# A memset behind every indirect DMA of GpSimd, and source rows taken from PSUM in one step of a graph network

## What is computed

```python
h = relu(layernorm(x)); x = x + L0(h)   # sum of h[src] * edge_weight * weight per destination
h = relu(layernorm(x)); x = x + L1(h)   # bilinear messages of dst rows and 8 edge features, silu, summed by source
h = relu(layernorm(x)); x = x + L2(h)   # 16x16 matrix of the edge's relation (90) times h[src], times a scalar
h = relu(layernorm(x)); x = x + L3(h)
# L3:
w = (gelu(gelu(edge_attr @ W1 + b1) @ W2 + b2) @ W3 + b3).reshape(-1, 16, 16)
for i in range(4):
    msg = einsum('ei,eio->eo', nodes[src], w)
    nodes = gelu(segment_sum(msg, dst) * inv_deg + nodes @ root_W[i] + root_b[i])
```

## Time and profile before

| what | value |
|---|---|
| median of 3 runs | 23921.9 us |
| the profiled execution | 23937.52 us |
| its span, first to last instruction | 23935.6 us |
| mean granted clock of TensorE | 0.931 |
| instructions | 398,392 |
| PE busy | 20518.6 us (86%) |
| POOL busy | 18138.0 us (76%) |
| DVE busy | 17386.4 us (73%) |
| ACT busy | 14285.8 us (60%) |

### The profile page before, as it was taken

The page is one execution under the profiler, slowest core; times in us unless marked ns, Lnnn a source line. Parts: engine busy times, 40 slices in busy tenths (PEclk is TensorE's granted clock), DMA queues, the critical chain, the costliest instruction groups (busy, mean ns, idle before and its releaser), DMA issues. The chain is left out here.

```text
span 23935.6 us, 398392 instructions
## 1 busy us (share of the span) xinstructions
PE 20518.6 (86%) x109882; PEld 11859.6 (50%) x109882; DVE 17386.4 (73%) x29340; ACT 14285.8 (60%) x24676; POOL 18138.0 (76%) x17163
## 2 busy tenths in 40 slices
PE   7999668888887999996888888699996999879997
PEld 4555345555555666663444444344443444434443
DVE  6555468888887999994555555588886888868886
ACT  7888611111112666663444444488886888878886
POOL 6777778888886777777777777777777777777777
PEclk9999879999998999998998899899998999989998
DMA  3222235555553223332333333366665666656665
GB/s 104 42 43 42 42 76 94 94 94 94 94 93 76 79 78 79 79 76 91 113 114 112 115 114 115 118 200 200 199 200 155 200 201 200 194 161 200 200 200 151
DMA packets 2201224, 2951.16 MB, mean 123 GB/s; under 512 B 782486, under 2 KB 1686884, under 8 KB 2199588
## 3 DMA queue, kind: packets, MB, share of 16 engines
q1 hardware_dynamic: 1340898, 2758.80, 35.2%
q0 software_dynamic: 790944, 162.36, 9.5%
q10 hardware_dynamic: 69282, 28.92, 0.5%
HBM read 2275.75 MB, written 672.64 MB: 123 GB/s over the span
## 5 line engine op out<-in xcount | busy, mean ns | idle before, releaser
L772 POOL DMA_INDIRECT got<-table,idx x14310 | 13886.3, 970 | 4697.2 <-issue 4166.5
L788 PE MATMUL in_place<-place_hot,tparts 128*128 128x512 fp8e4 (+1 forms) x49950 | 10826.1, 375 | 1229.7 <-ACT place_hot L993 1225.6
L993 ACT ACTIVATE place_hot<-place_b,far_lanes 128x512 fp8e4<-128x512 f16 (+1 forms) x17550 | 10584.3, 683 | 9.1 <-PE in_place L788 9.0
L788 PEld LDWEIGHTS in_place<-place_hot,tparts 128*128 128x128 bf16 x49950 | 4905.3, 100 | 6515.0 <-issue 1645.5
L1597 POOL DMA_INDIRECT added<-rows,add_idx x2160 | 3600.4, 1667 | 714.3 <-issue 655.8
L1169 DVE TENSOR_TENSOR prod<-w_in,rows_p 128x2048 f32<-128x2048 f32 x810 | 1853.0, 2288 | 1010.2 <-ACT rows_p L981 972.0
L1640 PE MATMUL acc<-hot,spread 128*128 128x392 bf16 x12960 | 2531.2, 349 | 0.0
L1214 DVE TENSOR_TENSOR prod<-wcopy,got 128x1024 f32<-128x1024 f32 x810 | 983.7, 1230 | 1840.7 <-DMA got<-table,idx 1303.3
L1223 DVE TENSOR_REDUCE msg<-prod 128x64 f32<-128x1024 f32 x1620 | 1967.8, 1215 | 41.3
L1182 DVE TENSOR_REDUCE msg<-prod 128x128 f32<-128x2048 f32 x810 | 1853.1, 2288 | 105.5
L857 PE MATMUL wmat<-k,h 128*128 128x256 f32 x6480 | 1797.6, 402 | 0.0
(11 more groups left out here) (249 smaller groups left out, 21238.2 us busy)
## 6 DMA issues: line engine op xcount, KB each, us to landing
w_in<-kept SPq DMA_DIRECT2D x2430, 512.0 KB
kept<-wcopy SPq DMA_DIRECT2D x810, 512.0 KB, 2.6
got<-table,idx POOLq DMA_INDIRECT x14310
attr<-in_edge_attr SPq DMA_DIRECT2D x270, 768.0 KB
place_b<-place_row SPq DMA_DIRECT2D x1080, 128.0 KB
range_b<-range_row SPq DMA_DIRECT2D x1080, 128.0 KB
rows<-in_src_row SPq DMA_DIRECT2D x270, 512.0 KB
sums<-outb SPq DMA_DIRECT2D x1350, 96.0 KB
```

The source lines that it names most:

```text
L772: pool.indirect_dma_start(out=got[:, r, j * W:(j + 1) * W], out_offset=None, in_=table, in_offset=bass.IndirectOffsetOnAxis(ap=idx[:, r, j ...
L788: mm = pe.matmul(in_place[b][:, h, :], tparts[:, s, t, :], place_hot[:, b, t, h * XC:(h + 1) * XC], start=(t == 0 and s == 0), stop=(t == ...
L993: ins = act.activation(place_hot[:, b, t, :], place_b[:, b, :], ACT.Abs_reciprocal_sqrt, bias=SB["far_lanes"][:, t:t + 1], scale=HOT_SLOPE ...
```

## The change

POOL clears one column of a scratch tile `spacer` behind each indirect DMA at lines 772, 1597 and 1917, a column of its own for each within the ring; before it begins a chunk whose columns were used before, it waits on `spaced` for those memsets. In "kernel_net" ACT copies the 12 gathered rows of a chunk to one PSUM tile, `rows_p`, after the chunk's second `copy_out`; DVE's products read that tile; POOL waits for `rows_made` in place of `got_used`. The bank comes from `h2p`, which has one buffer instead of two, so `layer2` waits for the gelu of the group just before.

```diff
+        spacer = sb("spacer", [P, RING * J0])
...
-            h2p = [ps(f"h2p{k}", [P, GE]) for k in range(2)]
+            h2p = ps("h2p", [P, GE])
+            rows_p = ps("rows_p", [P, 512])[:, 0:J0 * W]
...
                     if at is None or at >= RING:
-                        if kind == "kernel_kept":
+                        if kind in ("kernel_net", "kernel_kept"):
                             pool.wait_ge(S["rows_made"], k - RING + 1)
                         else:
                             pool.wait_ge(got_used[r], q)
                     pool.wait_ge(S["idx_made"], k + 1)
 
+                    if at is None or at >= RING:
+                        pool.wait_ge(S["spaced"], k - RING + 1)
                     pool.sem_inc(S["turn_open"], 1)
                     for j in range(J0):
                         pool.indirect_dma_start(
...
+                        ins = pool.memset(spacer[:, r * J0 + j:r * J0 + j + 1], 0.0)
+                    ins.then_inc(S["spaced"], 1)
...
-                    pe.wait_ge(S["h2_ready"], i * TURN_GROUPS + n + 1)
-                    pe.matmul(h2p[n % 2][:, :], SB["k2"][:, :], h1[:, n % 2, :], start=True, stop=True).then_inc(S["h2_made"], 1)
+                    pe.wait_ge(S["h2_ready"], i * TURN_GROUPS + n + 2)
+                    pe.matmul(h2p[:, :], SB["k2"][:, :], h1[:, n % 2, :], start=True, stop=True).then_inc(S["h2_made"], 1)
...
+                    def rows_over(k, r, q, first):
+
+                        act.wait_ge(got_in[r], (q + 1) * (16 * J0))
+
+                        if not first:
+                            act.wait_ge(w_used, k * GROUPS + 2)
+                        act.activation(rows_p, got[:, r, 0:J0 * W], ACT.Copy).then_inc(S["rows_made"], 1)
+
+                    def turn(i, odd, q, first):
...
                             copy_out(i, n, first)
+                            b, g = divmod(n, GROUPS)
+                            if g == 1:
+                                rows_over(i * HALVES + b, odd * HALVES + b, q, first and b == 0)
...
-                    dve.wait_ge(got_in[r], (q + 1) * (16 * J0))
+                    if kind == "kernel_net":
+                        dve.wait_ge(S["rows_made"], k + 1)
+                        rows_x = rows_p.rearrange("p (j f) -> p j f", f=W)
...
-                            bcast(rows_v[:, g * G:(g + 1) * G, 0:D], 2, D), ALU.mult).then_inc(w_used, 1)
+                            bcast(rows_x[:, g * G:(g + 1) * G, 0:D], 2, D), ALU.mult).then_inc(w_used, 1)
...
-                    dve.sem_inc(got_used[r], 1)
+                    if kind == "relational":
+                        dve.sem_inc(got_used[r], 1)
...
+        spacer = sb("spacer", [P, HALVES * ADDED])
...
+                        if at is None or at >= HALVES:
+                            pool.wait_ge(S["spaced"], k - 1)
                         for tables in (range(0, half), range(half, ADDED)):
...
                                     in_=add_rows[:, b, y * D:(y + 1) * D], in_offset=None, compute_op=ALU.add).then_inc(added[y], 16)
+                                ins = pool.memset(spacer[:, b * ADDED + y:b * ADDED + y + 1], 0.0)
+                        ins.then_inc(S["spaced"], 1)
...
+        spacer = sb("spacer", [P, NQ])
...
                         in_offset=bass.IndirectOffsetOnAxis(ap=SB["node_at"][:, q:q + 1], axis=0)).then_inc(all_in, 16)
+                    pool.memset(spacer[:, q:q + 1], 0.0)
```

More of the change, by code:

```diff
@@ L647, in edge_pass @@
                  "attr_used0", "attr_used1", "w_made", "w_used", "h1_made", "h1_ready", "h2_made", "h2_ready",
-                 "hot_made", "hot_used", "out_made", "stored0", "stored1", "dve_step", "run_cleared", "turn_open", "fetch_open",
+                 "hot_made", "hot_used", "out_made", "stored0", "stored1", "dve_step", "run_cleared", "spaced", "turn_open", "fetch_open",
                  "place_in0", "place_in1", "range_in0", "range_in1", "places_hot", "in_place_made", "picked_made", "in_row_made", "fetched",
@@ L931, in gelu2 @@
                         act.wait_ge(w_made, i * TURN_GROUPS + n + 1)
-                        act.activation(h2[:, n % 2, :], h2p[n % 2][:, :], ACT.Gelu_apprx_tanh, bias=SB["b2"][:, 0:1]).then_inc(S["h2_ready"], 1)
+                        act.activation(h2[:, n % 2, :], h2p[:, :], ACT.Gelu_apprx_tanh, bias=SB["b2"][:, 0:1]).then_inc(S["h2_ready"], 1)
                     def copy_out(i, n, first):
@@ L945, in copy_out @@
                         act.activation(wcopy[:, g, :], wmat[n % 2][:, :], ACT.Copy).then_inc(S["w_copied"], 1)
-                    def turn(i, first):
+                    def rows_over(k, r, q, first):
[4 more added lines that the diff above has]
+                    def turn(i, odd, q, first):
                         last = TURN_GROUPS
@@ L957, in turn @@
                             copy_out(i, n, first)
-                    turns(act, turn)
+                            b, g = divmod(n, GROUPS)
+                            if g == 1:
+                                rows_over(i * HALVES + b, odd * HALVES + b, q, first and b == 0)
+                    turn(0, 0, 0, True)
+                    with act.Fori(0, TURNS // 2) as q:
+                        turn(q * 2 + 1, 1, q, False)
+                        turn(q * 2 + 2, 0, q + 1, False)
                     return
@@ L1202, in matrix_chunk @@
                         c.step(dve.tensor_reduce(esum[:, :], eprod[:, :].rearrange("p (j f) -> p j f", f=D), AX, ALU.add))
-                    dve.wait_ge(got_in[r], (q + 1) * (16 * J0))
+                    if kind == "kernel_net":
+                        dve.wait_ge(S["rows_made"], k + 1)
+                        rows_x = rows_p.rearrange("p (j f) -> p j f", f=W)
+                    else:
+                        dve.wait_ge(got_in[r], (q + 1) * (16 * J0))
+                        rows_x = rows_v
                     def product(g):
@@ L1516, in edge_pass_scatter @@
         names = ["attr_in0", "attr_in1", "st_in0", "st_in1", "src_in0", "src_in1", "turned", "mask_made", "filled", "repeated", "xrep_made", "outer_made",
-                 "msg_made", "silu_made", "cut", "spread_made", "hot_made", "scattered", "same_made", "same_summed", "rows_made",
+                 "spaced", "msg_made", "silu_made", "cut", "spread_made", "hot_made", "scattered", "same_made", "same_summed", "rows_made",
                  "dve_step", "turn_open", "lower_made", "taken_out", "turned_p", "turned_s", "out_stored", "out_back",
```

## The result

The changed kernel takes 23707.99 us (median of 4 runs, 23703.14 to 23728.93) against 23922.14 for the kernel before (4 runs): a ratio of 0.9915, 95% interval 0.9903 to 0.9926. That is 214 us or 0.9% less, where 927 us or 3.9% less was forecast. It lies in the range of 22,250 to 24,800, but near none of the cases that had much chance: it is beside the third rival, "it hides and gives nothing". That it lies in the range at all is luck: the ends of the range come from the two wide rivals, and neither happened. The profiled execution took 23706.92 us, its span 23705.0.

What follows compares the result with a forecast made beforehand. POOL's indirect DMAs, with 0.30 us idle before each, were taken to bound the stages. From 23937.5 us, 829 for the memsets, 99 for the row copy and 16 for the profiled run's excess came off: 22,995 us, range 22,250 to 24,800.

Steps and rivals of the forecast that it cites:

- the third rival: Between indirect DMAs: the memset changes nothing within 7 ns, leaving the row copy's 99 us, 23,825 us; chance 0.09.
- the two wide rivals: Between indirect DMAs: memset simply added (24,785 us at the middle, chance 0.34), or taking the whole hand-over (22,380, chance 0.21).
- POOL's rows fill the stages: All stages: indirect DMAs plus 0.30 us idle each fill POOL's time, e.g. 2689 us of a 2705 us stretch.
- The memset's hand-over, 0.24 in place of 0.30: Between indirect DMAs: 0.07 + 0.10 + 0.07 us replaces 0.30, 0.06 less for 13818 of them, 829 us less.
- the slower rival: Between every two indirect DMAs: the hand-over remains and the memset adds 0.03 to 0.10 us, 24,240 to 25,380; chance 0.34.
- The estimate of 42 ns: GpSimd cores: each memset's dispatch charged 50 cycles at 1.2 GHz, 42 ns, giving 24,400 us.
- The gathers held by the product: Last layer's first step: with rows in PSUM gathers fall from 1022 to 945 ns, 250 us off POOL's time.
- The loop of 31.1 us, so only 99 us: Last layer's first step: the loop from attr through PE and ACT limits a turn to 31.1 us, 99 us less.
- The row copy on ACT: Last layer's first step: ACT's 128 x 192 copy behind the second group's copy-out takes 0.32 us.
- "nothing": Last layer's first step: ACT's wait for gathers and single-buffered h2p each cost nothing while the loop is the bound.

Runs made afterwards that it cites:

- experiment 8: Kernel before with only 8 of the 12 gathers of each chunk in the last layer's first step, the other places reading zeros: 23237.68 us.
- experiment 7: Changed kernel without memsets, plus the relational pass's mask in PSUM, mask and in_row single-buffered, weighted masks in PSUM too: 23701.16 us, ratio 0.9925.
- the early row copy: Changed kernel without memsets, 8 of 12 gathers a chunk in the last layer's first step, rows copied behind the first copy-out, not the second: 23189.74 us.

## Why the prediction failed, step by step

- **POOL's rows fill the stages: right.** Eight memsets make the kept steps 3067 us in place of 2705 (2160 x 0.16 = 346 of the 362), and a stage moved with one DMA's period wherever the others had room. One reading beside it was wrong and without effect: PE isn't the busiest engine of each stage, in the relational one DVE is (2885.10 against 2875.20 us).
- **The memset's hand-over, 0.24 in place of 0.30: this step failed.** It is the one that the prediction called its weakest, and it carries 829 of the forecast's 927 us; the memsets alone made 17 more. Its three terms were 0.07 + 0.10 + 0.07; measured are 0 + 0.12 + 0.19. The stretch between two gathers stayed 0.305. The error was to read the idle 0.30 as a hand-over that gets shorter when a simple instruction stands in it. The row itself spoke for a fixed interval: 0.30 behind 0.94 and behind 1.72 alike, which the prediction used only for the slower rival. The two readings "a memset fits into it" and "a memset is added" both follow from a fixed interval, and only the first is true up to two memsets. The first had a chance of 0.09, as a band of 7 ns between two wide cases; a fixed interval that hides what stands in it is a mechanism, not a thin band, and should have had a chance like the others.
- **Both pages that were weighed.** By "Perfetto Trace Analysis", section "GPSIMD Engine Instruction", of the Trainium skill, time is read from start to start; done so, the runs show 1.249 with none, one and two memsets, while the idle time shown fell by 1580 us. The advice held, but the conclusion drawn from it (nothing can hide in the 0.30) did not. The estimate of 42 ns by "GPSIMD Engine Reference", section "Instruction dispatch", stands beside 28 ns measured for each memset beyond the interval, and 0 within.
- **The gathers held by the product: right.** 1022 ns were forecast to become 945; 948 was measured, 238 us of the 250.
- **The loop of 31.1 us, so only 99 us: this step failed too, in size.** Measured: a turn of 30.07 and 238 us less. The prediction had 30.0 from the gathers and set it aside for a loop that it read off one turn. In that turn PE waited 5.28 us for `attr`; over the 134 turns behind the first it waited 3.7 on average. And the times of ACT's copies, taken as given, follow from PE's own work, which is slower behind such a wait. The windows of the kernel before around that turn (clock in the third column from the end):

```profile
13024.00:13034.00 10.00, 6.51 (x11) 3.06 (x12) 3.43 (x6) 1.37 (x2) 7.87 (x8) 0.53 0.21 62
13034.00:13044.00 10.00, 10.00 (x34) 5.82 (x33) 5.50 (x6) 4.80 (x6) 7.87 (x8) 0.96 0.36 120
13044.00:13054.00 10.00, 10.00 (x32) 5.07 (x31) 6.34 (x9) 6.39 (x8) 7.70 (x8) 1.00 0.50 177
13054.00:13064.00 10.00, 6.94 (x17) 3.34 (x16) 3.96 (x8) 2.83 (x4) 7.57 (x8) 0.74 0.21 63
```

  From inside PE's wait on the granted clock is 0.53 for 10 us, close to its lower level of 1.2 GHz; in the next 10 us it is 0.96, then 1.00. With 8 gathers PE hardly waits. PE's waits in the step, the kernel before first (us in total, times, longest; the first turn's is 145.3 of it), then with 8 gathers:

```profile
PE h1p L894 <- DMA attr<-in_edge_attr: 646.8, 135, 145.3
PE h1p L895 <- DMA attr<-in_edge_attr: 43.9, 66, 1.1
```

  The clock is at its lower level for 849 us of the step before and for 306 us with 8 gathers, its mean goes from 0.90 to 0.96, and PE's busy time for the same 11,340 matmuls from 3789 to 3563 us (the window shown in experiment 8 holds 11,258 of them, 3535 us). The loop shrinks with the wait that it was read from.
- **The row copy on ACT: right in price** (0.33 us, 0.32 forecast), and "nothing" held at 12 gathers: ACT waits for them 98 times, 109 us in all, and PE 24 us for ACT's first gelu ahead of `h2p`, but gathers alone fill the turn. With 8 gathers the copy's place costs 1.1 us a turn and `h2p` 0.1.
- **The rivals.** The slower one, at 0.34, has its mechanism, but only beyond 0.305: with four memsets 24,284, with eight 26,100. The 78 us that came from the products' changed start, and the 16 to 21 us by which memsets lengthen two stages, stood in no case.

## What to carry to other kernels

An interval before an instruction that stays the same whatever stands ahead of it may be a fixed one: small work put into it is free until it is full, and gives nothing, so price it at nothing first. Where a DMA issued by GpSimd takes longer than its fellows, see which DVE instruction it starts beside: one operand in PSUM may free it, but look for the next instruction that will hold it. Of a wait put down to an engine, take off the fixed interval first. A floor is not read off one turn in which another engine waits: change what it waits for, or compare many turns, since the wait and the clock behind it are part of the time read.

## What was not expected of the hardware

- Between two indirect DMAs of GpSimd lie 0.305 us, with 0, 1 or 2 one-column memsets in it. A memset starts as the DMA ends, takes 0.12, each further one 0.028, and the next DMA starts 0.15 to 0.16 behind the last at the soonest.
- A gather that starts in a DVE product with both inputs in SBUF is held until the product ends (it takes longer by what was left of the product, less 0.127 us: 362 gathers in the trace before); one that starts in the product's first 0.03 us isn't.
- Behind a scattered addition the memset is shown as beginning before the addition has ended, as in the changed kernel (order of time):

```profile
5000.07 1.56 POOL L1626 DMA_INDIRECT added<-rows,add_idx  x1 [0.19 <-issue]
5001.06 0.70 POOL L1629 MEMSET spacer<- 128x1 f32 x1
5001.94 2.02 POOL L1626 DMA_INDIRECT added<-rows,add_idx  x1 [0.19 <-issue]
```

  The memset begins 0.99 into the addition and ends 0.13 behind it: 0.70 us shown, where the same memset takes 0.12 elsewhere. The spans are not the work.
- A `tensor_scalar` with one tensor in SBUF (`onehot`, f16 to bf16) held 190 gathers in experiment 7 in the same way, not only instructions with two. By the section of the Trainium skill named there such an instruction can take the shared ports in a faster mode; whether it ran in that mode no row shows.
- With 8 gathers the early row copy made the step 48 us faster than no copy at all. PE's busy time for the 11,340 matmuls is 3520 us in place of 3563, and the granted clock is at its lower level for 215 us of the step in place of 306; 91 us at half the clock are worth 45. Why the clock fell for less time is open.
